# Constant products on the matrix engine ahead of nine of its waits, in a three-layer macaron block

## The chip, the cores and the metric

The kernel is one program on one core of a Trainium2 chip. The metric is the device time of one execution in microseconds (us). TensorE (PE) multiplies matrices, VectorE (DVE), ScalarE (ACT) and GpSimd (POOL) do the rest, and SyncE (SP) issues most transfers. In the trace PEld is a weight load of PE, and PEclk is the clock that PE was granted, as a share of 2.4 GHz: 1.00 is 2.4 GHz and 0.50 is 1.2 GHz.

## The reference

The input is one sequence of 2048 tokens of width 128. Three layers run in turn, each on a layernorm of the residual x:

```python
x = x + 0.5 * ffn(layernorm(x))      # layer 0
x = x + attn(layernorm(x))           # layer 1
x = x + 0.5 * ffn(layernorm(x))      # layer 2
```

`attn` is causal attention with 16 heads of 8, rotary positions and an output projection. `ffn` is a whole block of its own: rmsnorm, the same kind of causal attention, a residual, a second rmsnorm, and a mixture of experts. There a router takes the two best of 8 experts for each token, and each expert computes `(silu(h @ w_gate) * (h @ w_up)) @ w_down` with an inner width of 448. All of it is float32.

## The kernel before, in words

One loop over three layers holds three blocks. At the end of a block all engines meet; two of the blocks are skipped by a branch in layer 1.

**The core block** is attention. `hn` (tile `onat`) holds the normalised tokens; PE turns them (line 770), projects them in four chunks of 512 tokens (lines 779 and 787), and DVE, POOL and ACT build the rotated operands, which go through memory and come back. PE then waits for DVE and ACT (lines 793 to 796) and runs a list of events that a planner in `core_schedule` wrote out. For each of four groups of heads and four chunks of queries these are: products from which DVE takes row maxima (`rowmax`, line 815, reduced at line 604), one small transpose (`maxout`), scores (line 861), exponentials on ACT (line 753), and weighted values (line 874). The scores use banks 0 to 3 of PSUM, the row maxima and other side work banks 4 to 6, the weighted values bank 7.

The last events of each layer belong to the last chunk. ACT copies the weighted values out (line 760). PE turns them (`normalise`, line 829), DVE divides them (lines 629 and 630), PE turns them back (`turn`, line 838), DVE copies them (line 638), PE projects them (`project`, line 846), and DVE adds the bias and the residual (lines 644, 652 or 660) and takes sums (line 655 or 664). Each step waits for the one ahead of it.

**The router block** (layers 0 and 2) starts with a square root on ACT (line 921). DVE scales 16 tiles of tokens (`h2`, line 942), PE turns them into banks 4 and 5 (line 899), ACT copies each four (line 924), and PE multiplies them with the router's weights into bank 6 (line 888, 8 columns). A long chain of small DVE instructions picks two experts, PE sums ranks (lines 907 and 908, bank 7), DVE goes on with its chain (lines 973 to 1030), and PE multiplies one-hot matrices into the lists of the slots (line 913, bank 4). DVE turns those into row numbers (lines 1036 to 1045).

**The expert block** (layers 0 and 2) runs 39 slots of 128 tokens. POOL gathers a slot's tokens (line 1068), PE turns them (line 1118), ACT copies (line 1162), PE does gate and up (line 1133), ACT and DVE activate (lines 1173 and 1212), PE turns (line 1142), ACT copies (line 1179), PE does down (line 1151), DVE copies out (line 1221) and POOL scatters (line 1078).

`ones` is a 128x128 float32 tile filled with 1.0 before the loop; only line 908 reads it. A float32 product stands in the trace as two PE instructions, a float32 transpose as one.

Of the kernel before, what the change touches and what calls it, by code (L numbers as in the profile page):

```python
# [18 lines left out]
NC = T // CH  # L19
# [147 lines left out]
def macaron_kernel(nc, x_in, w5, b4, vecs, wo_w, rope, router, w_gate, w_up, w_down, out):  # L167
# [50 lines left out]
    ones = sb("ones", [128, 128])  # L218
# [26 lines left out]
    ps = nc.alloc_psum_tensor("ps", [128, 8, CH], F32)  # L245
# [107 lines left out]
    chunks, events, _ = core_schedule()  # L353
# [41 lines left out]
        return ka[64:96, b, :, :].rearrange("p h t -> p (h t)").bitcast(F32)  # L395


    with nc.Block() as block:

        @block.sync  # L400
# [65 lines left out]
    with nc.Fori(0, NLAYER) as layer:  # L466

        with nc.Block() as block:
# [294 lines left out]
            def _(pe):  # L763
# [10 lines left out]
                for c in range(NC):  # L774
                    pe.wait_ge(tokens_copied, c + 1)
                    for w in range(4):
                        if c:
                            pe.wait_ge(terms_ready, 4 * (c - 1) + w + 1)
                        pe.matmul(ps[:, 2 + w, :], w5s[:, w, :], hT[:, c * CH:(c + 1) * CH],
                                  start=True, stop=True).then_inc(projected, 1)  # L780
# [9 lines left out]

                pe.wait_ge(terms_ready, 4 * NC)
                pe.wait_ge(values_ready, NC)
                mi = 0
                pe.wait_ge(wo_loaded, 16)
                for ev in events:
                    kind = ev[0]
                    if kind in ("rowmax", "maxout", "normalise", "turn", "project"):
                        bank = SB + mi % MB  # L800
                        if mi >= MB:
                            pe.wait_ge(filler_used, mi - MB + 1)
                        mi += 1
                    if kind == "rowmax":
                        _, j, qt, h0, some, kc, final = ev
                        g, c = chunks[j]
                        b = g % 2
                        if qt == 0 and h0 == 0 and (kc == 0 or c == 0):
                            pe.wait_ge(group_loaded[g] if g else chunk_loaded[c], 16 * 6)
                        tile = TPC * c + qt  # L810
                        n = min(CH, (tile + 1) * 128 - kc * CH)
                        diag = kc == c
                        for k in range(some):
                            dst = ps[:, bank, k * n:(k + 1) * n]
                            ins = pe.matmul(dst, qa[0:KROWS, b, h0 + k, tile * 128:(tile + 1) * 128],  # L815
                                            ka[0:KROWS, b, h0 + k, kc * CH:kc * CH + n], start=True, stop=not diag)
                            if diag:
                                ins = pe.matmul(dst[:, n - 128:n], identb[:, :], mask_rows[:, :],  # L818
                                                start=False, stop=True)
                        ins.then_inc(filler_ready, 1)  # L820
                    elif kind == "maxout":
                        j = ev[1]
                        pe.wait_ge(maxima_ready, j + 1)
                        pe.transpose(ps[0:16, bank, 0:128], mx[:, j % MD, :], identf[:, :]).then_inc(filler_ready, 1)
                    elif kind == "normalise":
                        j = ev[1]
                        pe.wait_ge(output_copied, j + 1)
                        for k in range(TPC):
                            ins = pe.transpose(ps[:, bank, k * 128:(k + 1) * 128],  # L829
                                               otf[:, j % 2, k * 128:(k + 1) * 128], identf[:, :])  # L830
                        ins.then_inc(filler_ready, 1)
                        written = mi
                    elif kind == "turn":

                        c = ev[1]
                        pe.wait_ge(filler_used, written)
                        for k in range(TPC):
                            ins = pe.transpose(ps[:, bank, k * 128:(k + 1) * 128], onat[:, TPC * c + k, :], identf[:, :])
                        ins.then_inc(filler_ready, 1)
                        written = mi  # L840
                    elif kind == "project":
                        c = ev[1]
                        pe.wait_ge(filler_used, written)
                        for k in range(TPC):
                            t = TPC * c + k
                            ins = pe.matmul(ps[:, bank, k * 128:(k + 1) * 128], hT[:, t * 128:(t + 1) * 128],
                                            wos[:, 0:D], start=True, stop=True)
                        ins.then_inc(filler_ready, 1)
                    elif kind == "scores":
                        _, s, j, kt, h = ev  # L850
                        g, c = chunks[j]
                        b = g % 2
                        if kt == 0 and h == 0:
                            pe.wait_ge(guard_ready[j % MD], 16 * (j // MD + 1))
                        q0 = max(0, kt - TPC * c) * 128
                        n = CH - q0
                        u = HPG * s + h
                        if u >= SB:
                            pe.wait_ge(probs_ready, u - SB + 1)
                        dst = ps[:, u % SB, 0:n]  # L860
                        pe.matmul(dst, ka[0:KROWS, b, h, kt * 128:(kt + 1) * 128],  # L861
                                  qa[0:KROWS, b, h, c * CH + q0:(c + 1) * CH],
                                  start=True, stop=True).then_inc(scores_ready, 1)
                    elif kind == "values":
                        _, s, j, kt = ev
                        g, c = chunks[j]
                        q0 = max(0, kt - TPC * c) * 128
                        pe.wait_ge(probs_ready, HPG * (s + 1))
                        if kt >= TPC * c:
                            pe.wait_ge(masked, masks_to(j, kt))  # L870
                        if kt == 0 and j >= 1:
                            pe.wait_ge(output_copied, j)
                        for h in range(HPG):
                            ins = pe.matmul(ps[32 * h:32 * h + HD + 1, SB + MB, q0:CH],  # L874
                                            vv[:, kt, g * HPG + h, :], probs[:, s % 2, h, 0:CH - q0],
                                            start=kt == 0, stop=kt == TPC * (c + 1) - 1)
                        ins.then_inc(values_weighted, 1)


        with nc.Block() as block:  # L880

            @block.tensor
            def _(pe):
                with pe.If(layer != 1):
                    def logits(c):
                        pe.wait_ge(h2_copied, c + 1)
                        for t in range(TPC * c, TPC * (c + 1)):
                            ins = pe.matmul(ps[:, 6, t * E:(t + 1) * E], hT[:, t * 128:(t + 1) * 128], rts[:, :],
                                            start=True, stop=True)
                        ins.then_inc(logits_ready, 1)  # L890

                    pe.wait_ge(weights_loaded, 64)
                    for c in range(NC):
                        if c >= 2:
                            pe.wait_ge(h2_copied, c - 1)
                        for k in range(TPC):
                            t = TPC * c + k
                            pe.wait_ge(h2_ready, t + 1)
                            ins = pe.transpose(ps[:, 4 + c % 2, k * 128:(k + 1) * 128], h2[:, t, :], identf[:, :])
                        ins.then_inc(h2_turned, 1)  # L900
                        if c:
                            logits(c - 1)
                    logits(NC - 1)

                    pe.wait_ge(taken_ready, 1)
                    taken = gw[:, 5, :, :].rearrange("p t e -> p (t e)")
                    pe.matmul(ps[:, 7, 0:TT * E], below[:, :], taken, start=True, stop=True)
                    pe.matmul(ps[:, 7, TT * E:2 * TT * E], ones[:, :], taken, start=True, stop=True).then_inc(ranks_ready, 1)
                    pe.wait_ge(moves_ready, 1)
                    for q in range(NK // 8):  # L910
                        pe.wait_ge(places_ready, q + 1)
                        for k in range(8 * q, 8 * q + 8):
                            ins = pe.matmul(ps[:, 4, 0:NSLOT], places[:, k, :], moves[:, k, :],
                                            start=k == 0, stop=k == NK - 1)
                    ins.then_inc(slots_ready, 1)

            @block.scalar
            def _(act):
# [139 lines left out]
        with nc.Block() as block:  # L1058
# [54 lines left out]
            def _(pe):  # L1113
# [4 lines left out]
                    pe.transpose(ps[:, 7, 0:128], xring[:, u % XR, 0:D], identf[:, :]).then_inc(tile_turned, 1)  # L1118

                with pe.If(layer != 1):  # L1120
                    turn(0)
                    experts = []
                    for i in range(NSLOT + 2):
# [185 lines left out]
```

## Time and profile before

| | |
|---|---|
| three runs | 1900.51, 1901.65, 1904.47 us; median 1901.65 |
| profiled execution | 1902.52 us, its span 1900.9 us |
| mean granted clock over the span | 0.911 |
| PE busy | 1678.3 us (88%) |
| DVE busy | 1379.6 us (73%) |
| ACT busy | 1073.4 us (56%) |
| POOL busy | 444.9 us (23%) |

The span runs from the first to the last instruction on the core; the execution's own time is 1.6 us more. The busy share is a mean over all stages and hides the stretches that this change is about, in which PE mostly waits. A row of the timeline gives start, length, engine, line and what was written from what, the number of merged instructions, and in brackets how long the engine had stood idle and who ended that. A row of the windows gives a stretch, its length, the busy time of each engine in it with its number of instructions, the granted clock, and the share and rate of the DMA engines.

### The profile page before, as it was taken

Reading aid. Unit: us, or ns where it says so; the run is one execution under the profiler, and the core shown is the slowest. Engines: PE = TensorE matmul, PEld = TensorE weight load, DVE = VectorE, ACT = ScalarE, POOL = GpSimd, SP = SyncE. Lnnn points to the kernel's source line nnn. Section 1 sums busy time; section 2 is a strip of 40 time slices with the busy share of each in tenths; the row PEclk is TensorE's granted clock in tenths of the full one; section 3 lists DMA queues with packets and bytes.
Section 4 is the critical chain, followed back from the end, with each engine's and each line's share of the span. In section 5 each row is a group of like instructions: output and inputs, shape, how many; then the busy total and the mean of one; then the engine's idle time right before and its main releaser. Section 6 shows DMA issues by size and latency. Waiting matters only on the chain. (4 is left out here: it accounts for less than half of the span.)

```text
span 1900.9 us, 30318 instructions
## 1 busy us (share of the span) xinstructions
PE 1678.3 (88%) x10566; PEld 720.8 (38%) x10566; DVE 1379.6 (73%) x2863; ACT 1073.4 (56%) x2301; POOL 444.9 (23%) x492
## 2 busy tenths in 40 slices
PE   4799999999749948899999999579999999993995
PEld 2333333333237723233333332233333333323674
DVE  8788899987153348888999983388899999826333
ACT  2355677677614413356777678234576777781442
POOL 6300201111016637000102020260011010200664
PEclk9788999999859967889999999678899999995898
DMA  4500203300011134200202000242002020001113
GB/s 130 118 21 3 51 3 99 71 2 2 8 33 41 43 103 139 52 1 2 52 2 52 3 2 2 60 139 52 2 12 42 2 52 2 2 2 30 38 43 88
DMA packets 63574, 75.83 MB, mean 40 GB/s; under 512 B 13655, under 2 KB 56220, under 8 KB 62104
## 3 DMA queue, kind: packets, MB, share of 16 engines
q1 hardware_dynamic: 54184, 62.13, 13.1%
q0 software_dynamic: 4992, 9.40, 2.0%
q10 hardware_dynamic: 4224, 2.10, 0.4%
q8 instruction: 95, 1.56, 0.4%
q14 instruction: 79, 0.65, 0.1%
HBM read 53.05 MB, written 21.46 MB: 39 GB/s over the span
## 5 line engine op out<-in xcount | busy, mean ns | idle before, releaser
L753 ACT ACTIVATE probs<-ps 128x512 f32<-128x512 f32 (+3 forms) x1920 | 879.1, 542 | 473.0 <-PE ps L861 471.6
L604 DVE TENSOR_REDUCE mpart<-ps 128x1 f32<-128x512 f32 (+3 forms) x1680 | 1015.1, 666 | 117.3 <-PE ps L815 65.5
L815 PE MATMUL ps<-ka,qa 96*128 96x512 bf16 (+3 forms) x1920 | 669.9, 371 | 36.4 <-DMA ka<-ksplit 23.6
L861 PE MATMUL ps<-qa,ka 96*128 96x512 bf16 (+3 forms) x1920 | 616.1, 357 | 3.1 <-DMA qa<-guard 2.5
L874 PE MATMUL ps<-probs,vv 128*9 128x512 f32 (+3 forms) x3840 | 441.8, 532 | 8.8 <-ACT probs L753 8.1
L702 POOL TENSOR_SCALAR_AFFINE_SELECT probs<-probs 128x512 f32<-128x512 f32 x192 | 121.8, 634 | 1180.0 <-ACT probs L753 1180.0
L815 PEld LDWEIGHTS ps<-ka,qa 96*128 96x128 bf16 x1920 | 191.9, 100 | 480.7 <-DVE mpart L604 338.6
L861 PEld LDWEIGHTS ps<-qa,ka 96*128 96x128 bf16 x1920 | 183.6, 100 | 189.0 <-ACT probs L753 69.2
L818 PE MATMUL ps<-mask_rows,identb 128*128 128x128 bf16 x768 | 161.4, 235 | 0.0
L1212 DVE SCALAR_TENSOR_TENSOR probs<-probs,slot_w,ps 128x448 f32<-128x448 f32 x78 | 53.1, 680 | 117.2 <-PE ps L1133 113.7
L874 PEld LDWEIGHTS ps<-probs,vv 128*9 128x9 f32 x3840 | 57.7, 88 | 157.8 <-ACT probs L753 116.4
L1068 POOL DMA_INDIRECT arena<-tokens,from_row x78 | 76.9, 985 | 115.7 <-issue 69.5
L1078 POOL DMA_INDIRECT results<-hT,to_row x78 | 78.5, 1007 | 74.2 <-issue 42.1
L629 DVE RECIPROCAL rden<-ps 128x16 f32<-128x16 f32 x48 | 12.1, 251 | 112.5 <-PE ps L829 111.9
L818 PEld LDWEIGHTS ps<-mask_rows,identb 128*128 128x128 bf16 x768 | 80.2, 104 | 29.2 <-issue 2.5
L1151 PE MATMUL ps<-wds,probs 112*128 x624 | 82.8, 275 | 1.4 <-DVE hT L1221 1.2
L1151 PEld LDWEIGHTS ps<-wds,probs 112*128 112x128 f32 x624 | 75.8, 192 | 2.3 <-issue 2.3
L1133 PE MATMUL ps<-wgs,hT 128*128 x156 | 74.8, 562 | 0.8 <-ACT hT L1162 0.5
L1179 ACT ACTIVATE probs<-ps 112x512 f32<-112x512 f32 x78 | 46.6, 597 | 51.1 <-PE ps L1142 51.1
L1133 PE MATMUL ps<-wus,hT 128*128 x156 | 73.6, 555 | 0.0
L1162 ACT ACTIVATE hT<-ps 128x128 f32<-128x128 f32 x78 | 21.7, 278 | 78.7 <-PE ps L1118 78.7
L770 PE MATMUL ps<-identf,onat 128*128 128x128 f32 x48 | 9.1, 321 | 63.1 <-DVE onat L557 63.1
(170 smaller groups left out, 1092.8 us busy)
## 6 DMA issues: line engine op xcount, KB each, us to landing
qa<-qsplit SPq DMA_DIRECT2D x27, 384.0 KB
ka<-ksplit SPq DMA_DIRECT2D x27, 384.0 KB
probs<-rope SPq DMA_DIRECT2D x12, 512.0 KB, 6.7
qa<-qsplit SPq DMA_DIRECT2D x36, 96.0 KB
ka<-ksplit SPq DMA_DIRECT2D x36, 96.0 KB
qsplit<-arena SPq DMA_DIRECT2D x6, 384.0 KB, 3.2
ksplit<-arena SPq DMA_DIRECT2D x6, 384.0 KB, 2.8
tokens<-arena SPq DMA_DIRECT2D x2, 1024.0 KB, 7.4
```

The costliest lines, as they stand in the source:

```text
L604: dve.tensor_reduce(mpart[:, j % MD, h0:h0 + some, qt, kc], ps[:, bank, 0:some * w].rearrange("p (h w) -> p h w", h=some), axis=AX.X, op=A ...
L702: pool.affine_select(out=own, in_=own, compare_op=ALU.is_ge, fill=0.0, base=0, pattern=[[0, HPG], [1, 128]], channel_multiplier=-1).then_i ...
L753: act.activation(probs[:, s % 2, h, 0:n], ps[:, u % SB, 0:n], ACT.Exp, scale=SCALE).then_inc(probs_ready, 1)
L815: ins = pe.matmul(dst, qa[0:KROWS, b, h0 + k, tile * 128:(tile + 1) * 128], ka[0:KROWS, b, h0 + k, kc * CH:kc * CH + n], start=True, stop= ...
L818: ins = pe.matmul(dst[:, n - 128:n], identb[:, :], mask_rows[:, :], start=False, stop=True)
L861: pe.matmul(dst, ka[0:KROWS, b, h, kt * 128:(kt + 1) * 128], qa[0:KROWS, b, h, c * CH + q0:(c + 1) * CH], start=True, stop=True).then_inc( ...
L874: ins = pe.matmul(ps[32 * h:32 * h + HD + 1, SB + MB, q0:CH], vv[:, kt, g * HPG + h, :], probs[:, s % 2, h, 0:CH - q0], start=kt == 0, sto ...
L1068: pool.indirect_dma_start(xring[:, u % XR, :], None, tokens, bass.IndirectOffsetOnAxis(ap=from_row[:, u:u + 1], axis=0)).then_inc(tile_loa ...
L1078: pool.indirect_dma_start(results, bass.IndirectOffsetOnAxis(ap=to_row[:, u:u + 1], axis=0), obuf[:, u % OR, :], None, bounds_check=TOPK * ...
L1133: pe.matmul(ps[:, 2 * (i % 2) + k, 0:M], xt[:, i % 2, :], w[:, bass.ds(expert, 1), :].rearrange("p o m -> p (o m)"), start=True, stop=True ...
L1151: ins = pe.matmul(ps[:, 6, 0:D], atb[u % 2][:, k, :], wds[0:MR, bass.ds(experts[u], 1), k, :].rearrange("p o d -> p (o d)"), start=k == 0, ...
L1212: dve.scalar_tensor_tensor(acb[i % 2], sgb[i % 2], slot_w[:, i % XR:i % XR + 1], ps[:, 2 * (i % 2) + 1, 0:M], ALU.mult, ALU.mult).then_inc ...
```

## The change

A helper `spin(pe, n)` issues n blocks of 128 columns of products of `ones` with itself, at most 512 columns in one instruction, into bank 0 of PSUM. Nobody reads what they write. It is called at ten places, one of them with n = 0. No wait, no other instruction and no order of the other work is changed.

```diff
+    def spin(pe, n):
+        wide = ones[:, :].rearrange("p (o c) -> p o c", o=1)
+        for k in range(0, n, 4):
+            m = min(4, n - k)
+            pe.matmul(ps[:, 0, 0:m * 128].rearrange("p (o c) -> p o c", o=m), ones[:, :],
+                      wide.broadcast_to([128, m, 128]), start=True, stop=True)
...
+                spin(pe, 12)
                 pe.wait_ge(terms_ready, 4 * NC)
...
                     elif kind == "normalise":
                         j = ev[1]
+                        if j == len(chunks) - 1:
+                            spin(pe, 2)
                         pe.wait_ge(output_copied, j + 1)
...
                         c = ev[1]
+                        if c == NC - 1:
+                            spin(pe, 2)
                         pe.wait_ge(filler_used, written)
...
                     elif kind == "project":
                         c = ev[1]
+                        if c == NC - 1:
+                            spin(pe, 2)
                         pe.wait_ge(filler_used, written)
...
                         ins.then_inc(values_weighted, 1)
 
+                spin(pe, 8)
...
                     pe.wait_ge(weights_loaded, 64)
+                    spin(pe, 6)
                     for c in range(NC):
...
                     logits(NC - 1)
 
+                    spin(pe, 0)
                     pe.wait_ge(taken_ready, 1)
...
+                    spin(pe, 40)
                     pe.wait_ge(moves_ready, 1)
...
                     ins.then_inc(slots_ready, 1)
+                    spin(pe, 2)
...
                 with pe.If(layer != 1):
+                    spin(pe, 8)
                     turn(0)
```

The first five calls run in every layer, the others in layers 0 and 2.

## Rows read from the trace of the kernel before

**Rows 1.** Timeline, tail of the last chunk of layer 0.
```profile
510.33 0.41 PE L874 MATMUL ps<-probs,vv 128*9 128x128 f32 x8 [0.22 <-POOL probs L702]
510.79 0.60 ACT L760 ACTIVATE otf<-ps 128x512 f32<-128x512 f32 x1 [1.31 <-PE ps L874]
...
511.54 0.63 PE L829 MATMUL ps<-identf,otf 128*128 128x128 f32 x4 [0.80 <-ACT otf L760]
...
513.00 1.09 PE L838 MATMUL ps<-identf,onat 128*128 128x128 f32 x4 [0.84 <-DVE onat L630]
...
515.02 2.04 PE L846 MATMUL ps<-wos,hT 128*128 128x128 f32 x8 [0.94 <-DVE hT L638]
...
520.40 0.18 DVE L938 TENSOR_SCALAR rst<-rst 128x16 f32<-128x16 f32 x1 [0.61 <-PEq L468]
```

**Rows 2.** Windows around the tail, and one of layer 1's first group.
```profile
505.00:509.00 4.00, 3.47 (x27) 0.95 (x25) 0.00 (x0) 3.27 (x11) 1.56 (x3) 1.00 0.00 0
509.00:513.00 4.00, 1.66 (x21) 0.75 (x21) 0.55 (x2) 1.08 (x4) 0.98 (x2) 0.97 0.00 0
513.00:517.00 4.00, 3.06 (x12) 2.46 (x12) 0.75 (x1) 0.00 (x0) 0.00 (x0) 0.50 0.31 82
...
837.00:840.50 3.50, 2.51 (x25) 1.03 (x21) 3.43 (x6) 1.02 (x5) 1.27 (x2) 1.00 0.02 5
```

**Rows 3.** Timeline of PE: projections, in layers 0 and 2.
```profile
36.51 1.06 PE L787 MATMUL ps<-otf,hT 128*128 128x128 f32 x8
37.45 3.70 PE L779 MATMUL ps<-hT,otf 128*128 128x512 f32 x8
...
50.60 0.26 PE L815 MATMUL ps<-ka,qa 96*128 96x128 bf16 x1 [8.56 <-DMA ka<-ksplit]
...
1223.45 6.72 PE L779 MATMUL ps<-hT,otf 128*128 128x512 f32 x8 [0.78 <-ACT hT L723]
```

**Rows 4.** Windows at the rise of layer 2's projections, and after layer 0's.
```profile
1229.00:1229.60 0.60, 0.60 (x2) 0.09 (x2) 0.60 (x1) 0.00 (x0) 0.44 (x1) 0.53 0.00 0
1229.60:1230.00 0.40, 0.40 (x2) 0.13 (x1) 0.13 (x1) 0.00 (x0) 0.00 (x0) 1.00 0.07 20
41.00:45.00 4.00, 1.05 (x9) 0.85 (x7) 4.00 (x5) 2.38 (x4) 4.00 (x5) 1.00 0.59 192
45.00:50.00 5.00, 0.00 (x0) 0.00 (x0) 3.60 (x3) 3.47 (x6) 4.82 (x4) 0.51 0.89 191
```

**Rows 5.** Timeline and window, router block of layer 0.
```profile
522.17 4.30 DVE L942 SCALAR_TENSOR_TENSOR arena<-x,rst,vbc 128x128 f32<-128x128 f32 x16
...
522.67 2.23 PE L899 MATMUL ps<-identf,arena 128*128 128x128 f32 x8 [5.61 <-DVE arena L942]
...
524.69 1.72 PE L888 MATMUL ps<-rts,hT 128*128 128x8 f32 x8
...
533.06 0.29 DVE L954 TENSOR_REDUCE gs<-ps 128x16 f32<-128x128 f32 x1 [6.59 <-PE ps L888]
...
522.60:533.10 10.50, 10.35 (x48) 9.78 (x48) 3.91 (x16) 3.67 (x5) 0.00 (x0) 0.50 0.44 100
```

**Rows 6.** Timeline, lists of layer 0.
```profile
549.80 0.45 PE L913 MATMUL ps<-arena,probs 128*128 128x39 f16 x8 [11.60 <-DVE arena L1030]
...
553.21 0.45 PE L913 MATMUL ps<-arena,probs 128*128 128x39 f16 x8 [0.69 <-DVE probs L1020]
```

**Rows 7.** Timeline and windows, start of the expert block of layer 0.
```profile
555.77 2.50 DVE L1195 SCALAR_TENSOR_TENSOR x<-x,xs 128x512 f32<-128x512 f32 x4 [0.39 <-PEq L880]
...
559.79 0.48 PE L1118 MATMUL ps<-identf,arena 128*128 128x128 f32 x1 [6.14 <-DMA arena<-tokens,from_row]
...
561.97 1.86 PE L1133 MATMUL ps<-wgs,hT 128*128 x2 [0.53 <-ACT hT L1162]
...
561.90:567.40 5.50, 5.43 (x8) 2.63 (x9) 0.76 (x3) 2.31 (x4) 2.82 (x3) 0.50 0.21 48
```

## Prediction

> **What bounds the kernel now.** I read the page first (PE busy 88%), then the granted clock in windows of 10 us over the whole span, then windows of 1 us and the timeline where it was 0.50, then the waits there. For most of the span PE is busy and at 2.4 GHz, and these streams don't touch that. The change can matter only where PE's work sits on the chain at 1.2 GHz. There are four such places.
>
> The first is the tail of each core block. It is a ping-pong, in which PE's steps and those of DVE and ACT alternate and every one is on the path [rows 1]. The clock was 1.00 to 512.9 us, after 4 us in which PE was busy for only 1.66 us, and 0.50 from there [rows 2]. So the first four transposes took 0.63 us, the next four, of the same shape, 1.09 us, and the projection 2.04 us [rows 1]. Layers 1 and 2 show the same to 0.02 us. The second is the router block up to the logits: PE busy 10.35 of 10.5 us, all at 0.50, and DVE waits for it [rows 5]. The third is the lists, where PE waits 11.60 us for DVE's chain [rows 6]. The fourth is the start of the expert block: PE waits 6.14 us for a gather and then works 5.4 us at 0.50 [rows 7].
>
> **Price of a stream.** Four float32 products of 512 columns took 3.70 us at 1.00, the last 0.2 us or so of it latency, so one takes 0.87 us, and four took 6.72 us when the clock rose only at 1229.6, so one takes 1.68 us [rows 3, 4]. A block of 128 columns is thus 0.22 us at 2.4 GHz and 0.42 us at 1.2 GHz. That the streams' weights are constant should change nothing in this.
>
> **Tail (2, 2, 2, 8), three layers.** PE waits 0.80, 0.84 and 0.94 us there [rows 1]. A stream of 2 costs 0.43 us at full clock and 0.84 us at half clock; it fits at full clock and just about fits at half, so it delays at most a few hundredths. With two of them in 509 to 513 us PE is busy 1.66 + 0.87 = 2.5 of 4 us. The nearest row is 2.51 of 3.5 us, where the clock was 1.00 throughout [rows 2]; the row of the fall has 1.66. Our 2.5 lies nearer the former. In 513 to 517 us there follow the transposes, a stream, the projection and the stream of 8, with little idle time between them. I take it that the clock holds until the projection is done. Then the second transposes cost 0.63 us [rows 1] and the projection costs 1.06, by the eight products of the same shape in the projections [rows 3]: 0.46 + 0.98 = 1.44 us less for each layer, and 4.3 us in all. Not at all held, it is 0. Half held (to 515 us) it is 3 x 0.46 = 1.4.
>
> The stream of 8 behind it takes 1.74 us at full clock; between the projection's end (517.06) and the next block's start (520.40) lie 3.3 us of DVE's residual and sums, so it is hidden. At half clock it takes 3.4 us, from 517.06 to 520.4, just where the next block started [rows 1]: between 0 and 0.4 us late for each layer. With the clock held, 0.
>
> The saving goes through DVE and the block's end to everything behind it: the router in layers 0 and 2, the turn of the loop in layer 1.
>
> A rule of the Trainium skill speaks against the first step. "TensorE: Matmul & The Clock Gate", Part 4 (PE-mode transpose), says that transposes don't count as busy for the clock as other products do. No row here has transposes alone at length to test it. By it, half of what PE does between 509 and 515 us would hold nothing up, only the streams would, and the fall could come before the projection; that is the second rival below.
>
> **Ahead of the first row maxima (12), three layers.** It takes 2.6 us in a wait of 8.56 us [rows 3], so it costs nothing. Some 6 us stay idle behind it. After the projections of layer 0, 4 us with 1.05 us of PE work had the clock at 1.00 and the next 5 us without any had it at 0.51 [rows 4]. So it falls again before the first product. Gain 0; at best a fraction of a us.
>
> **Ahead of h2 (6), two layers.** The block starts at about 520.35 and the first transpose at 522.67 [rows 1, 5], a gap of 2.3 us. The stream takes 1.3 us at full clock, and 2.5 us at half, which is 0.2 us late; PE is the bound there, so this is kept: +0.2 us for each layer. Against it stands a clock that is up for part of the stretch. If it were up for all of it, the end would be that of DVE's 16 tiles (526.5), the last transposes 0.6, ACT's copy 0.6 and half of 1.72 for the last logits, 528.6 instead of 533.03: 4.4 us for each layer [rows 5]. I don't expect it, because 10.35 busy us of exactly this work left the clock at 0.50 [rows 5], and the stream stands before it and not in it. In some executions the clock will be up for the first few us, where DVE sets the pace anyway. I take -0.2 us for each layer as the balance of both, -0.4 in all. Bounds: +0.4 and -8.8.
>
> **Lists (40 and 2), two layers.** Ten products at 1.68 us are 16.8 us, too long for the 11.60 us [rows 6]. But products of this very shape raised the clock at 1229.6, 6.1 us after the first of them [rows 3, 4]. With 6.1 us at half clock (3.6 products) and 6.4 x 0.87 = 5.6 at full, the ten take 11.7 us: 0.1 us late. That is absorbed, since the four batches of line 913 are 1.13 us apart on DVE and take PE 0.45 each [rows 6]. At full clock the last batch may end 0.1 us earlier. The 2 blocks behind run beside DVE's row numbers. Gain 0.
>
> **First slot (8), two layers.** From the block's start at 555.7 to the first transpose at 559.8 there are 4.1 us [rows 7], and the stream takes 3.4 us at half clock, so it delays nothing. Behind it come 2.2 us with two small transposes, then the dense work that the low clock doubles. For a gain the clock would have to rise during the stream and hold across these 2.2 us. That would be worth half of the 5.4 us, 2.7 for each layer and 5.4 in all [rows 7]. In the rows so far a rise took 5.4 us or more of continuous work (561.97 to 567.4) [rows 7]. I take 0.
>
> **The sum.** -4.3 (tail) - 0.4 (h2) and 0 for the rest: -4.7 us against the profiled execution's own 1902.52 us, 1897.8. That execution lies 0.9 us above the median of the three runs, 1901.65. It also fell early in the tail, and other executions may have fallen later and have less to win. Against the median I take -4.4: 1897.2 us.
>
> **Rivals.**
>
> *More stretches than the tail get the clock* (h2, the first slot, or both in part). For it: both streams stand directly ahead of PE-bound work, where full clock is worth 8.8 and 5.4 us. Against it: 10.35 us of busy time that didn't raise it [rows 5], and 2.2 us of near idleness behind the last stream [rows 7]. With half of both it is 1897.2 - 7 = 1890 us.
>
> *The tail isn't held.* For it: the streams are only 0.87 us in 4, and the idle gaps remain. Then the stream of 8 at half clock ends the block 0.2 us late in three layers (0.6), h2 starts 0.2 us late in two (0.4), and if the fall comes between the second transposes and the projection, 1.4 are won: 1901.65 + 1.0 - 1.4 = 1901.3 us, no change.
>
> *The 40 blocks stay at half clock,* the slower side. This is one mechanism at one place: the stream starts at 549.80 - 11.60 = 538.2 and ends 16.8 us later at 555.0. The four batches of line 913 take 1.8 us on PE and ended at 553.66 [rows 6], so the stream costs something once it ends after 551.9, which is when the clock rises later than some 10 us into it. All at half clock, the batches end at 556.8: +3.1 us for each layer, 6.3 in two. A clock that ignores these products gains nothing in the tail either, and h2 is 0.2 us late twice: 1901.65 + 6.3 + 0.4 = 1908.3 us. Against it: the same shape raised the clock in every layer's projections.
>
> **How the numbers follow.** The forecast, tail alone, has 0.52; more stretches 0.20; tail not held 0.21; the 40 blocks 0.05; and 0.02 is left for a cost that I don't see, such as fetching some 90 more PE instructions a layer. 0.2% is 3.8 us, about what a measurement of this kernel can tell from no change, and the three runs themselves are 4.0 us apart. Of the forecast's 0.52 some 0.37 lie beyond 3.8 us and 0.15 within it. Faster: 0.37 + 0.20 = 0.57. Same: 0.15 + 0.21 = 0.36. Slower: 0.07. The range takes in half of what h2 and the first slot could give on one side and the tail that isn't held on the other: 1889.5 to 1902.5. The forecast's own range is 1895 to 1900.
>
> **What the profile after would show.** Right: lines 838 and 846 of the last chunk at about 0.63 and 1.06 us in all three layers, clock 1.00 up to the projection's end; line 899 starting 1.4 us sooner after line 829; the router's stretch still near 10 us at mostly 0.50; the clock rising within the 40 blocks and line 913 starting when DVE has its operands; gate and up of the first slot still at twice their length. Wrong: a fall between lines 829 and 846; a router stretch well under 10 us; a first gate and up of 0.9 us; line 913 waiting for its own engine. What I may have wrong above all is how much work holds the clock, since it rests on two rows, and whether each execution falls at the place where this one did.

## The result, and the profile after

The changed kernel takes 1888.93 us (median of 4 runs, 1887.67 to 1890.54), the one before 1901.08 (4 runs, 1900.13 to 1904.47). The ratio is 0.9932, its 95% interval 0.9917 to 0.9948. That is 12.2 us less, where 4.4 were forecast, and 0.6 us below the low end of the range. The profiled execution's span is 1889.0 us, 11.9 less than before, with a mean granted clock of 0.93 instead of 0.911.

In the kernel after, line 402 is the product of `spin`. Lines 839, 850 and 860 are the last chunk's `normalise`, `turn` and `project` (829, 838, 846 before), 915 and 903 turn h2 and multiply with the router's weights (899, 888), and 973 is the first DVE step on the logits (954). Timeline of layer 0, tail and router, the counterpart of [rows 1, 5]:

```profile
510.29 0.41 PE L888 MATMUL ps<-probs,vv 128*9 128x128 f32 x8 [0.22 <-POOL probs L709]
...
510.63 0.70 PE L402 MATMUL ps<-ones 128*128 128x256 f32 x2
...
511.41 0.66 PE L839 MATMUL ps<-identf,otf 128*128 128x128 f32 x4
...
511.90 0.60 PE L402 MATMUL ps<-ones 128*128 128x256 f32 x2
...
512.81 0.66 PE L850 MATMUL ps<-identf,onat 128*128 128x128 f32 x4 [0.31 <-DVE onat L637]
...
514.31 1.16 PE L860 MATMUL ps<-wos,hT 128*128 128x128 f32 x8 [0.41 <-DVE hT L645]
...
515.30 1.88 PE L402 MATMUL ps<-ones 128*128 128x512 f32 x4
...
518.89 1.55 PE L402 MATMUL ps<-ones 128*128 128x512 f32 x4 [1.71 <-PEq L475]
...
520.99 2.17 PE L915 MATMUL ps<-identf,arena 128*128 128x128 f32 x8 [0.54 <-DVE arena L961]
...
522.99 0.96 PE L903 MATMUL ps<-rts,hT 128*128 128x8 f32 x8
...
525.56 2.73 PE L903 MATMUL ps<-rts,hT 128*128 128x8 f32 x16
...
528.32 0.29 DVE L973 TENSOR_REDUCE gs<-ps 128x16 f32<-128x128 f32 x1 [3.45 <-PE ps L903]
```

Windows of the same stretch (columns as in [rows 2]):

```profile
509.00:513.00 4.00, 2.94 (x26) 1.47 (x27) 0.55 (x2) 1.04 (x4) 0.94 (x2) 1.00 0.00 0
513.00:517.00 4.00, 3.59 (x18) 2.07 (x17) 1.92 (x3) 0.00 (x0) 0.00 (x0) 1.00 0.30 82
...
521.00:526.40 5.40, 5.40 (x40) 4.53 (x40) 3.87 (x15) 2.42 (x5) 0.00 (x0) 1.00 0.09 27
526.40:528.30 1.90, 1.88 (x10) 1.79 (x9) 0.00 (x0) 1.25 (x1) 0.00 (x0) 0.50 1.06 270
```

The turn and the projection are at their full-clock lengths. More important, the clock is still up when the router block starts. It stays up for 5.4 us of the very work that ran at 0.50 for 10.35 us before [rows 5] and falls at 526.4, with only the last few logits left.

Lists and first slot (lines 931, 1137 and 1153, the counterpart of [rows 6, 7]):

```profile
533.25 10.43 PE L402 MATMUL ps<-ones 128*128 128x512 f32 x20
545.06 0.37 PE L931 MATMUL ps<-arena,probs 128*128 128x39 f16 x8 [1.38 <-DVE arena L1049]
...
551.14 3.77 PE L402 MATMUL ps<-ones 128*128 128x512 f32 x4 [1.20 <-PEq L895]
555.04 0.48 PE L1137 MATMUL ps<-identf,arena 128*128 128x128 f32 x1
556.34 0.47 PE L1137 MATMUL ps<-identf,arena 128*128 128x128 f32 x1 [0.81 <-DMA arena<-tokens,from_row]
557.30 1.86 PE L1153 MATMUL ps<-wgs,hT 128*128 x2 [0.49 <-ACT hT L1182]
558.95 1.70 PE L1153 MATMUL ps<-wus,hT 128*128 x2
...
560.59 0.92 PE L1153 MATMUL ps<-wgs,hT 128*128 x2
```

The 40 blocks end 1.38 us before the operands are there. The first gate and up still run at twice their length; the clock rises 3.2 us after they begin, where it took 5.4 before.

Where the 11.9 us went, by times between fixed points of the two timelines, in us:

| stretch | before | after | gained |
|---|---|---|---|
| last values to projection's end, layers 0, 1, 2 | 6.33 each | 4.77 each | 4.7 |
| last values to first h2 transpose, layers 0, 2 (includes the row above) | 11.94 each | 10.29 each | 0.2 beyond it |
| first h2 transpose to logits seen by DVE | 10.39 each | 7.34, 7.33 | 6.1 |
| logits seen to first slot's transpose | 26.73, 26.69 | 26.72, 26.61 | 0.1 |
| first slot's transpose to slot 2's output | 17.54, 17.42 | 16.53, 16.45 | 2.0 |
| all else | | | -1.1 |

"All else" holds the attention of the three layers (496.50, 494.81, 495.35 before; 496.47, 493.58, 496.22 after, from a layer's start to its last values, 0.4 us gained in all), the two turns of the loop (0.2 and 0.7 longer) and the end (0.6 longer). It is the difference of two profiled executions and not a price of the change: the attention of one layer alone differs by up to 4 us between the kernels below that leave it as it is.

### The profile page after: what moved, and what is told of

It reads as the page before. It is cut to its first block and busy times, and to the rows that moved or that the text cites. A ratio compares the mean times of both kernels' runs of the same rounds, so it can differ in the third digit from the quotient of the medians.

```text
span 1889.0 us, 30523 instructions
## 1 busy us (share of the span) xinstructions
PE 1718.1 (91%) x10674; PEld 730.5 (39%) x10674; DVE 1379.2 (73%) x2863; ACT 1073.5 (57%) x2301; POOL 445.3 (24%) x492
## 3 DMA queue, kind: packets, MB, share of 16 engines
q8 instruction: 95, 1.56, 0.4%
```

## The experiments

Each kernel is an edit of the changed one and was timed against the kernel before on the same chip. Where a call is gone, its n was set to 0. Four chips were used. On two of them the kernel before took 1901 to 1903 us; no_tail, no_lists, no_slot and no_first ran on a third, pair, three, through and start on a fourth, and on these two slower chips the kernel before took 1923 to 1924 us. So ratios are compared, and stretches within the trace. "Router" is the stretch from the first h2 transpose to the logits seen, "slot" that from the first slot's transpose to slot 2's output, each for layers 0 and 2. The chips differ in the slots (see the end), so the last column is compared only between kernels of the faster or of the slower chips; the others agree on all four.

| kernel | ratio | 95% interval | tail to projection's end | router | slot |
|---|---|---|---|---|---|
| before | 1 | | 6.33 | 10.39, 10.39 | 17.54, 17.42 |
| the change | 0.9932 | 0.9917 to 0.9948 | 4.77 | 7.34, 7.33 | 16.53, 16.45 |
| tail_only | 0.9969 | 0.9958 to 0.9980 | 4.77 | 10.38, 10.38 | 17.58, 16.61 |
| no_h2 | 0.9962 | 0.9948 to 0.9975 | 4.77 | 10.39, 10.38 | 16.60, 16.45 |
| no_end8 | 0.9947 | 0.9931 to 0.9963 | 4.77 | 7.38, 7.37 | 16.54, 16.44 |
| thin | 0.9984 | 0.9973 to 0.9995 | 6.14 | 10.47, 10.48 | 17.70, 17.57 |
| no_tail | 0.9974 | 0.9961 to 0.9986 | 5.88, 6.34, 6.34 | 9.82, 8.80 | 16.04, 16.71 |
| no_lists | 0.9948 | 0.9932 to 0.9963 | 4.77 | 7.34, 7.33 | 16.86, 16.75 |
| no_slot | 0.9943 | 0.9929 to 0.9957 | 4.77 | 7.33, 7.34 | 16.95, 16.70 |
| no_first | 0.9937 | 0.9922 to 0.9951 | 4.77 | 7.34, 7.34 | 17.62, 16.78 |
| pair | 0.9943 | 0.9929 to 0.9956 | 4.77 | 7.36, 7.35 | 17.50, 16.74 |
| three | 0.9964 | 0.9950 to 0.9977 | 4.77 | 10.40, 10.41 | 17.70, 16.65 |
| six_alone | 0.9996 | 0.9986 to 1.0006 | 6.33 | 10.28, 10.27 | 17.43, 17.30 |
| through | 0.9917 | 0.9903 to 0.9930 | 4.77 | 7.29, 7.34 | 15.94, 14.91 |
| start | 0.9890 | 0.9875 to 0.9905 | 4.77 | 7.33, 7.33 | 17.64, 16.85 |
| both | 0.9875 | 0.9861 to 0.9890 | 4.77 | 7.34, 7.33 | 14.81, 14.63 |
| both_rows | 0.9879 | 0.9865 to 0.9894 | 4.77 | 7.33, 7.33 | 14.78, 14.70 |

**tail_only**: all calls but the three streams of 2 are gone.

```diff
-                spin(pe, 12)
...
-                spin(pe, 8)
...
-                    spin(pe, 6)
...
-                    spin(pe, 40)
...
-                    spin(pe, 2)
...
-                    spin(pe, 8)
```

> Only the three streams of 2 in the tail are left; the stream of 8 at the core block's end and all others are gone. Three theories. Chain: a clock held in the tail is what carries the router block, and every link is needed, so without the 8 and the 6 the clock falls in the pause between the projection and h2; the tail keeps its 1.6 us a layer (values' end to the first h2 transpose 10.3 us where before has 11.9), the stretch from the first h2 transpose to the logits seen on DVE returns to about 10.4 us (7.3 with the whole change), and the time is 1901 - 4.8 = about 1896 us. Local: each stream works for the place behind it alone; the same here, 1896 us. Not the clock: streams help by keeping PE's queue busy; then the tail's steps keep their length of 1.09 and 2.04 us and the time stays at 1901.

1896.21 us, ratio 0.9969, which is 5.9 us less (3.8 to 8.0): 1.56 us a layer from the tail and the router untouched. The forecast's own sum of 4.4 us lies within that; this kernel is what the forecast described.

**no_h2**: the stream ahead of h2 is gone.

```diff
-                    spin(pe, 6)
```

> The whole change without the 6 blocks ahead of h2. Chain: the pause from the end of the 8 (517.2) to the first h2 transpose (521.0) is then without work, the clock falls in or soon after it, and the router's stretch is 9.5 to 10.4 us instead of 7.3: 4.5 to 6 us more than with the whole change, about 1894 us. Local: the same, since the 6 alone would make the router's gain. Carried by the 8 alone: the router's stretch stays near 7.3 us and the time near 1889.

The whole gain of the router is lost. Windows of no_h2, layer 0:

```profile
519.00:520.00 1.00, 0.09 (x1) 0.00 (x0) 0.97 (x8) 0.00 (x0) 0.00 (x0) 1.00 0.00 0
520.00:521.00 1.00, 0.00 (x0) 0.00 (x0) 0.27 (x3) 0.35 (x1) 0.00 (x0) 1.00 0.00 0
521.00:522.00 1.00, 0.00 (x0) 0.00 (x0) 0.00 (x0) 0.99 (x2) 0.00 (x0) 0.72 0.00 0
522.00:523.00 1.00, 0.02 (x1) 0.05 (x1) 0.77 (x3) 0.16 (x1) 0.00 (x0) 0.50 0.00 0
```

The tail and the 8 left the clock up, PE stood for 3.9 us, and the clock fell during that, 1.5 us before the first transpose at 522.98.

**no_end8**: the stream at the end of the core block is gone.

```diff
-                spin(pe, 8)
```

> The whole change without the 8 blocks at the end of the core block, the 6 ahead of h2 left in. Chain: about 3.5 us without work between projection and the 6; the clock falls there, the 6 start at half clock, and the router's stretch goes back to 9.5 to 10.6 us: about 1894 us. Local: the 6 alone make the router's gain, stretch 7.3 us, 1889 us.

I expected a loss; the router's stretch stayed at 7.38 us, as the local theory had it. But the timeline shows a third thing (here line 915 is the h2 transpose, as in the change):

```profile
519.34 2.28 PE L402 MATMUL ps<-ones 128*128 128x512 f32 x4 [3.43 <-PEq L475]
521.43 2.22 PE L915 MATMUL ps<-identf,arena 128*128 128x128 f32 x8
523.48 0.96 PE L903 MATMUL ps<-rts,hT 128*128 128x8 f32 x8
```

```profile
520.00:521.00 1.00, 1.00 (x4) 0.39 (x2) 0.25 (x1) 0.69 (x2) 0.00 (x0) 0.50 0.00 0
...
522.00:523.00 1.00, 1.00 (x5) 0.68 (x5) 1.00 (x5) 0.28 (x1) 0.00 (x0) 0.50 0.00 0
523.00:524.00 1.00, 1.00 (x9) 0.92 (x8) 1.00 (x5) 0.64 (x2) 0.00 (x0) 0.79 0.00 0
524.00:525.00 1.00, 1.00 (x11) 1.00 (x12) 1.00 (x5) 0.32 (x2) 0.00 (x0) 1.00 0.00 0
```

The clock fell while the 6 ran and rose again some 4 us after their start, with the 6 and eight transposes behind one another, in time for the logits. Layer 2 shows the same. So the 8 are not needed here, and there are two ways to the same gain: to hold the clock, or to raise it again just ahead of the work.

**thin**: every product of `spin` has 8 columns.

```diff
-            pe.matmul(ps[:, 0, 0:m * 128].rearrange("p (o c) -> p o c", o=m), ones[:, :],
-                      wide.broadcast_to([128, m, 128]), start=True, stop=True)
+            pe.matmul(ps[:, 0, 0:8], ones[:, :], ones[:, 0:8], start=True, stop=True)
```

> The same calls and the same number of product instructions, but each of 8 columns and not of up to 512; what they compute is read by nobody. If the gain is the clock, brought by the columns streamed, it is gone: clock 0.50 from some 2 us after the last values, 1901 us give or take 1. If it is the presence of instructions ahead of the waits, the gain of 12 us stays.

With as many instructions but few columns the router gains nothing and the clock falls as before. The tail is 0.19 us shorter a layer, and 0.9984 is just off 1, so about 3 us come with the mere instructions, or with chance. Tail of thin (lines 838, 849, 859 for the three steps):

```profile
512.54 1.11 PE L849 MATMUL ps<-identf,onat 128*128 128x128 f32 x4 [0.62 <-DVE onat L636]
...
514.50 2.08 PE L859 MATMUL ps<-wos,hT 128*128 128x128 f32 x8 [0.62 <-DVE hT L644]
```

```profile
509.00:513.00 4.00, 2.58 (x26) 1.75 (x27) 0.55 (x2) 0.78 (x3) 0.67 (x2) 0.93 0.00 0
```

PE's busy time is 2.58 of 4 us here, above the 2.5 that the prediction counted on, and the clock fell all the same; the change has 2.94. That alone leaves room for a border between the two. The change's own router doesn't: there the clock fell at 526.4 after PE had been busy for 5.40 of 5.40 us. So PE's busy time alone does not tell whether the clock holds.

**no_tail**: the three streams of 2 are gone.

```diff
-                            spin(pe, 2)
...
-                            spin(pe, 2)
...
-                            spin(pe, 2)
```

> The whole change without the three streams of 2 in the tail. Chain: the clock falls about 2 us after the last values as before, the projection takes 2.04 us, the 8 and the 6 find half clock; the tail's 4.8 us are lost and so are most of the router's 6.1, unless the 8 at half clock, which follow the projection without a gap, raise it again. 1898 to 1901 us without such a rise, 1892 to 1895 with it. Local: only the tail's part is lost, 1894 us.

The ratio of 0.9974 lies between the two numbers, 5 us gained. The tail is lost but for 0.45 us in layer 0, where the second transposes still took 0.63 us, and the router's gain is lost in part. In layer 0 the 8 followed the projection without a gap and the clock came up again:

```profile
516.00:519.00 3.00, 3.00 (x8) 1.47 (x7) 1.78 (x5) 0.00 (x0) 0.00 (x0) 0.65 0.00 0
519.00:522.00 3.00, 1.79 (x5) 0.68 (x4) 1.04 (x9) 1.50 (x2) 0.00 (x0) 1.00 0.00 0
...
525.00:528.00 3.00, 3.00 (x16) 3.00 (x16) 1.22 (x5) 0.73 (x2) 0.00 (x0) 0.50 0.24 73
```

**no_lists, no_slot, no_first**: one of the remaining calls each is gone (40 and 2; the last 8; the 12).

```diff
-                    spin(pe, 40)
...
-                    spin(pe, 2)
```

> The whole change without the 40 blocks and the 2 around the lists. Rows after show no gain from first ranks to first slot (26.7 us from the logits seen to the first slot's transpose, before and after), so the time stays at 1889 if that is all. If the 40 are what lets the clock rise sooner in the first slot (3.2 us after gate and up began, where before it took 5.4), 2 us are lost: 1891.

```diff
-                    spin(pe, 8)
                     turn(0)
```

> The whole change without the 8 blocks ahead of the first slot. If they bring the 1.0 us a layer from the first slot's transpose to slot 2's output (16.5 us instead of 17.5), that goes back to 17.5 and the time is about 1891. If the sooner rise is only where the changes of the clock happened to lie against the work, it stays: 1889.

```diff
-                spin(pe, 12)
                 pe.wait_ge(terms_ready, 4 * NC)
```

> The whole change without the 12 blocks ahead of the first row maxima. I hold them to be worth nothing, since about 6 us without work lie behind them: 1889 us, within 1. If they do help the first chunks, where the clock is at half for tens of us, some us are lost.

Ratios of 0.9948, 0.9943 and 0.9937 against 0.9932: none differs from the change beyond the intervals. The slot's stretch, for which the 8 were meant, is 16.95 and 16.70 us without them, and on the same chip 17.62 and 16.78 with them in no_first.

**pair**: the tail's streams and the 6, and nothing else.

```diff
-                spin(pe, 12)
...
-                spin(pe, 8)
...
-                    spin(pe, 40)
...
-                    spin(pe, 2)
...
-                    spin(pe, 8)
```

> Only the three streams of 2 in the tail and the 6 ahead of h2; the 12, both 8s, the 40 and the last 2 are gone. By the runs so far these four calls carry the whole gain: tail 1.6 and router 3.0 us a layer, the ratio 0.994 to 0.9945, as with the whole change within its interval (0.9917 to 0.9948). If the other five calls add something (the first slot, 1 us a layer), it is 0.995 to 0.9955.

0.9943: four calls of 2, 2, 2 and 6 have 5.7 of the 6.8 thousandths, and the rest is within the intervals. They don't get it by holding the clock. As in no_end8 it was up when the 6 began at 518.65 and fell at 519.3 while they ran, was down for most of the transposes (from 520.77), and was up again at 522.7, just ahead of the logits (522.77), in both layers:

```profile
521.00:522.00 1.00, 1.00 (x5) 0.72 (x4) 1.00 (x5) 0.00 (x0) 0.00 (x0) 0.50 0.00 0
...
523.00:524.00 1.00, 1.00 (x11) 1.00 (x11) 1.00 (x5) 0.57 (x1) 0.00 (x0) 1.00 0.00 0
```

**three**: half the stream ahead of h2.

```diff
-                    spin(pe, 6)
+                    spin(pe, 3)
```

> The whole change with 3 blocks ahead of h2 in place of 6. At full clock they take 0.65 us of a pause of 2.1 us behind the block's start. If the 6 only just hold the clock, the 3 don't, and the router's stretch goes back from 7.3 to 9 or 10 us, ratio about 0.996. If any stream there does, it stays at 7.3 us, ratio 0.993.

Half the stream brings nothing of the router's gain, even with the 8 in place. PE was busy for 1.27 us between 518 and 521 us, and for 1.57 in the change. The clock fell at 522.6, just as the logits began:

```profile
521.00:522.00 1.00, 1.00 (x5) 0.50 (x5) 1.00 (x5) 0.20 (x1) 0.00 (x0) 1.00 0.00 0
522.00:523.00 1.00, 1.00 (x7) 0.75 (x6) 1.00 (x5) 0.47 (x2) 0.00 (x0) 0.80 0.00 0
523.00:524.00 1.00, 1.00 (x6) 1.00 (x7) 1.00 (x5) 0.52 (x1) 0.00 (x0) 0.50 0.00 0
```

**six_alone**: the 6 ahead of h2 without any other call.

> Only the 6 blocks ahead of h2, nothing in the tail. Carried: the clock has fallen near the second transposes, the 6 run at 0.50 and take 2.5 us in a pause of 2.3, the router's stretch stays at 10.4 us or 0.2 more, and the ratio is 0.9995 to 1.0005. Local: the 6 and the eight transposes behind them, nearly 5 us of dense work, raise the clock; then the logits run at full clock, the stretch is 7.5 to 9 us, and the ratio is 0.998.

0.9996. The 6 found half clock, took 2.92 us and made the first transpose 0.5 us late (12.47 us after the last values, 11.94 before), and the clock never rose:

```profile
520.99 2.92 PE L402 MATMUL ps<-ones 128*128 128x512 f32 x4 [3.42 <-PEq L475]
523.70 1.91 PE L915 MATMUL ps<-identf,arena 128*128 128x128 f32 x8
...
522.00:527.00 5.00, 5.00 (x20) 3.96 (x19) 4.54 (x17) 1.54 (x4) 0.00 (x0) 0.50 0.00 0
```

So the 6 depend on the clock that the tail's streams leave. In no_end8 and pair, where the 6 started at full clock and were overtaken by the fall, it rose again, in both layers of each; here, in both layers, with as long a stretch of dense work, it didn't. Its 12 runs go from 1894.8 to 1904.5 us, wider than those of the change, so in some executions it may have risen. Only one was profiled.

**through**: the clock held from the ranks to gate and up.

```diff
-                    spin(pe, 40)
+                    spin(pe, 46)
...
                     for q in range(NK // 8):
+                        if q:
+                            spin(pe, 3)
                         pe.wait_ge(places_ready, q + 1)
...
-                    spin(pe, 2)
+                    spin(pe, 8)
...
-                    spin(pe, 8)
+                    spin(pe, 18)
                     turn(0)
+                    spin(pe, 3)
...
                         if i < NSLOT:
+                            if not i:
+                                spin(pe, 2)
                             expert = pe.value_load(eti[0:1, i:i + 1], min_val=0, max_val=E - 1)
```

> The change with longer streams from the lists to the first slot: 46 for 40, 3 blocks between the four batches of the lists, 8 for 2 behind them, 18 for 8 ahead of the first slot, 3 and 2 more around the second transpose, so that the clock never falls from the ranks to gate and up. If the low clock is what the first slot still pays for, the stretch from its transpose to slot 2's output falls from 16.5 to about 15.0 us, 3 us in two layers, ratio 0.9915. If a fall comes in the 1.2 us border between blocks all the same, the 18 run at half clock, end 2 to 3 us late, and the time is 1 to 5 us worse than the change.

0.9917 as expected, though the time alone can't tell it from the change's 0.9932, since the intervals overlap. The trace can: the slot's stretch is 15.94 and 14.91 us, where three, start and pair on the same chip have 17.5 to 17.7 and 16.65 to 16.85.

**start**: streams at the start of the core block, in bank 7.

```diff
+                spin(pe, 10, 7)
                 turn_tokens(0)
+                spin(pe, 2, 7)
                 for c in range(NC):
```

The third argument is the bank.

> The change and, at the start of each core block, 10 blocks ahead of the first turn and 2 ahead of the first projection, in bank 7. The first projections run at half clock there (6.7 us for four products; 3.7 at full). If PE is the bound in that stretch, 2 to 3 us a layer are won from the layer's start to the values' end, 6 to 9 us in all, ratio about 0.989. If DVE, POOL and the transfers behind set the first row maxima, nothing is won, and the ratio stays at 0.993.

0.9890, the largest single step found: layer start to last values takes 492.47, 493.01 and 493.30 us. Their sum is 1478.8 us (1479.2 in both); in the kernels without these streams it lies between 1483.0 and 1491.0. Layer 2 (lines 777 and 788, the turn and the projections, which took 6.72 us before [rows 3]):

```profile
1215.67 3.90 PE L402 MATMUL ps<-ones 128*128 128x512 f32 x6 [12.92 <-issue]
1219.53 1.10 PE L777 MATMUL ps<-identf,onat 128*128 128x128 f32 x4
1220.47 0.60 PE L402 MATMUL ps<-ones 128*128 128x256 f32 x2
1221.41 3.70 PE L788 MATMUL ps<-hT,otf 128*128 128x512 f32 x8 [0.34 <-ACT hT L730]
```

**both** and **both_rows**: through and start together; then 36 blocks for the 12.

```diff
-                spin(pe, 12)
+                spin(pe, 36)
                 pe.wait_ge(terms_ready, 4 * NC)
```

> The change with the longer streams through lists and first slot and the ones at the core block's start. If the two gains stand on different stretches, they add: about 0.989 - (0.9932 - 0.9917) = 0.9875 against before.

> The same with 36 blocks in place of 12 ahead of the first row maxima, 7.7 us at full clock in a wait of about 7.5 to 8.5 us. The first row maxima then begin at full clock. If PE's products bind that stretch, 1 to 3 us a layer are won, ratio 0.984 to 0.986. If DVE's reductions or the operands' transfers bind it, or the stream ends late in layers 1 and 2, where the wait is 1 us shorter, nothing is won or up to 1 us a layer lost: 0.9875 to 0.989.

both takes 1878.18 us, 0.9875, the number expected if the two gains add, and it is faster than the kernel before and than the change. Against start alone (0.9890) the intervals overlap. Its slot stretch is 14.81 and 14.63 us, 1.7 and 1.8 less than the change's, with the clock at 1.00 throughout:

```profile
545.00:551.00 6.00, 5.48 (x28) 2.44 (x28) 4.90 (x16) 0.00 (x0) 1.46 (x1) 1.00 0.00 0
551.00:555.00 4.00, 3.57 (x13) 1.57 (x11) 0.54 (x3) 0.87 (x3) 3.03 (x4) 1.00 0.18 50
555.00:561.00 6.00, 6.00 (x25) 3.61 (x26) 2.00 (x7) 3.74 (x8) 2.83 (x3) 1.00 0.22 44
```

both_rows adds nothing (0.9879), although its first row maxima do start at full clock, where those of both had 0.50:

```profile
48.00:52.00 4.00, 3.23 (x27) 1.50 (x25) 3.43 (x7) 0.71 (x1) 3.72 (x5) 1.00 0.87 243
52.00:56.00 4.00, 2.19 (x9) 0.55 (x8) 3.38 (x8) 0.00 (x0) 4.00 (x6) 0.72 0.96 318
```

DVE and POOL are busy there for 3.4 to 4.0 of 4 us, and PE soon waits (2.19 of 4 us busy).

## Why the prediction was wrong

**Right in sign and place, wrong in size.** The forecast was 1897.2 us, the result 1888.9. The likeliest case, the tail alone, is what tail_only measured (1896.2); the case that came true is the first rival, for which I had 0.20 and 1890 us.

**Price of a stream:** right by the column, but the sum left the end of a stream out. The 10 products of the lists took 10.43 us where 11.7 were reckoned, because the clock rose 3.4 us into them and not 6.1. A stream of 2 in the tail took 0.60 to 0.70 us where 0.43 were reckoned. At half clock the 8 ahead of the first slot took 3.77 us for 3.4, and the 6 of six_alone 2.92 for 2.5. So h2 was 0.5 us late in six_alone and not 0.2.

**Tail:** right, 1.56 us a layer measured and 1.44 forecast. But its argument was partly luck. It went by PE's busy time, 2.5 of 4 us; thin has 2.58 and the clock fell. The change in fact had 2.94 there, since its streams were longer than reckoned. The transposes and products between the streams, and the streams, all ran at full clock here. The Trainium skill's rule in "TensorE: Matmul & The Clock Gate", Part 4 (PE-mode transpose), that transposes don't count like products, didn't keep the clock from being held. Whether they counted at all no run here isolates.

**The 8 at the core block's end:** hidden, as forecast. No loss without them is shown either (no_end8).

**Ahead of h2, the step that failed.** "If it were up for all of it ... I don't expect it, because 10.35 busy us of exactly this work left the clock at 0.50." Measured: 3.05 us a layer instead of 0.2, 6.1 in all instead of 0.4, which is 5.7 of the 7.8 us missed. (4.4 us a layer were reckoned for a clock that stays up to the end; the last logits ran at half.) The row was read for more than it says. It shows that this work, started at the low level, doesn't *raise* the clock. It doesn't show that a clock which is up *falls* at once, and in the change it lasted through 5.4 us of that work, long enough for all but the last few logits. Nor does it show that a stream ahead of this work can't bring the clock back within it, which happened in no_end8 and pair. The same row of the tail [rows 2] could have warned: there too the clock outlived the dense work by some 2 us. And I priced each stream by itself. no_h2, tail_only and six_alone show that neither the tail's streams nor the 6 make the router's gain, and pair that both together do. The two parts interact; a sum of separate terms can't have it.

**Lists and the 12:** 0 forecast, and none shown in the runs (no_lists, no_first; both_rows for a stream three times as long).

**First slot:** 0 forecast, 1.0 us a layer in the profile after. No run shows that the stream brings it. In the change the clock rose 3.2 us after the first gate and up began, and in pair, which has no stream behind h2 at all, as early: its first gate and up take 1.85 and 1.67 us from 557.08, the next gate 0.92 from 560.34. The stretch has some 7.6 us of low clock in each layer before, 5.5 in the change, 5.4 and 5.6 in pair, and 5.6 and 5.5 in no_slot, which lacks the 8 alone. So it goes with the moment at which the clock happens to rise, and that moment was no worse without the stream. That a rise takes 5.4 us or more, as I had it from two rows, was wrong. My reason for the 0, idle time around two small transposes, held for this stream and fell once the idle time was filled too: 14.6 to 14.8 us in both.

**The rest:** layer 0's attention takes from 494.1 us (no_lists) to 498.4 (no_h2) in kernels that leave its start alone, and the loop's turns and the end move by up to 1.3 us too. The 1.1 us of loss in the ledger is of that size; why these stretches move is not shown.

**Slower side:** the rival of the 40 blocks was wrong; the clock rose early in them.

**Still open:** why six_alone didn't raise the clock where no_end8 and pair did, each known from one execution; and what the 3 us of thin are.

## What to carry to other kernels

Find the stretches in which PE is on the chain at the low clock, and judge fillers by stretches in a row, not one at a time. A clock that is up is worth keeping over a short pause, since it may outlast dense work that did not raise it itself. Try the length of the stream, and where it stands: half of a sufficient one (three) was worth nothing, while 3.4 us of pause ahead of the 6 could stay empty (no_end8, pair), and a stream that starts at the low clock can be a little late (six_alone). Read the granted clock after, too: in the change the router's gain came by a clock that held, in no_end8 and pair by one that fell and came back. And look for PE-bound work right behind a long wait; here the largest gain (start) was at a place that the change left out.

## What the runs showed of the hardware

Constant products of ones raise the clock like others: 3.4 us after the first of the 40 blocks it was at 1.00. As many instructions with 8 columns each don't hold it in the tail: PE was busy for 2.58 of 4 us with them (thin) and for 2.94 with the wide ones.

The clock can fall while PE has no idle time: at 526.4 in the change it did, after 5.40 of 5.40 us busy with transposes of 128 columns and products of 8.

Two chips ran the kernel before in 1901.5 and 1902.7 us, two others in 1923.4 and 1923.7. About 20 us of the difference are in the expert block: from slot 2's output to slot 38's it is 103.5 to 103.6 us for each layer on the first two and 113.1 to 114.6 on the others, while tail, router and lists agree to about 0.1 us. The first slots are longer there too: with 5.5 us of low clock the slot's stretch is 16.4 to 16.5 us on the first two (the change, no_end8) and 16.7 to 17.6 on the others (no_lists, no_slot, no_first). In that block the slower chips' traces show waits that end "remote", which those of the first two don't have there, for DVE alone 7 in 70 us (waits of no_first, 590 to 660 us):

```profile
DVE probs L1232 <- remote: 19.4, 7, 3.4
```

What they are was not looked into.
